# The first batch of an attention and mixture-of-experts kernel goes through the prologue in two halves

## The chip, the cores and the metric

The kernel runs on one core of one Trainium2 chip. The metric is the device time of one execution in microseconds (us), from the program's start to its end; the profile's span is the part of it from the first to the last instruction.

## The reference, cut to what matters

Four batches of 512 rows of 128 numbers go through a layernorm, an attention in segments, a projection and a layernorm with a residual, and then through a layer of eight experts (two per row) and a shared one.

```
B, M, D = (4, 512, 128)      H = 16, hd = 8, SEG = 128, DIL = 2, S = M // SEG = 4
qkv = layernorm(x) @ w_qkv.T
q, k, v = split by head, rows reordered by perm (a snake of width 23)
kd, vd = every second key and value of each segment of 128        # 64 keys a segment
scores = einsum('bhsqd,bhskd->bhsqk', q * hd**-0.5, kd)
attn   = softmax(scores);  o = einsum('bhsqk,bhskd->bhsqd', attn, vd)
x = x + layernorm(o @ w_out.T)
x = x + layernorm(moe(layernorm(x)))      # router, top 2 of 8 experts, shared gated expert
```

## The kernel before

Each engine has a program of its own, an order written out by hand, and semaphores tie them together. The work comes in three parts: a prologue that brings batch 0 (and the projections of batch 1) to the point where the attention can begin, a loop of three stages i = 0, 1, 2, in which the attention of batch i runs interleaved with the query scores of batch i + 1 and the projections of batch i + 2, and then the attention of batch 3 with the experts of all batches.

What a batch needs before its attention, in the names of the code:

- VectorE (DVE) takes the statistics of the four row tiles (`stats_x`: `bn_stats`, `bn_aggr`, one add), GpSimd (POOL) raises them to the power of -1/2 (`powers`), DVE makes the scaled negative mean (`neg_mean`), ScalarE (ACT) normalises the tiles (`normalise_x`, tile `XN`).
- TensorE (PE) transposes them (`x_T`). The products run in a number format that rounds its inputs, so each operand is split into a high part, copied by ACT (`x_high`, tile `xTh`), and a low part, the rest, subtracted by DVE (`x_low`, `xTl`); `split3` adds three products. `qkv` makes queries and keys, which are split again (`qk_high`, `qk_low`: `qch`, `qcl`, `kch`, `kcl`).
- `select_k` and `select_q` multiply by a 0/1 matrix `sel` and lay high and low parts of a group of four heads one under the other; ACT copies the results to `Ks` and `Qs` (`k_rows`, `q_rows`, one of the four query groups by DVE). DVE masks the keys by head into `Kb` (`k_blocks`, four instructions).
- `scores_q` gives scores whose row maxima DVE takes (`maxima`, tile `negm`); `max_split` splits them into `Mq`, PE transposes (`max_T`), ACT and DVE copy them into rows 96 to 127 of `Qs` (`max_rows`), where rows of `Kb` filled with ones (`kone`, made by ACT, spread by eight DMAs) meet them in `scores_k`. Its results are already less the maximum, and ACT takes the exponential (`exps`). `values` and `v_blocks` bring the values to `Vb`, `attend`, `attend_T` and `divide` end the attention.
- POOL copies every second column of `xTh` and `xTl` for the values (`key_columns`), and subtracts for the low parts of some weights (`w_low`: `rwl`, `gul`, `w1l`).

The order of DVE in the prologue is: statistics of batch 0, low part of the weights, `neg_mean(0, 0)`, the two copies to `sel`, statistics of batch 1, `x_low(0)`, `neg_mean(0, 1)`, `qk_low(0)`, two copies that put the ones into `Vb`, `k_blocks(0)`, statistics of batch 2, `q_rows(0)`, `maxima(0, 0)`, `neg_mean(0, 2)`, `x_low(1)`, `maxima(0, 1)`, `qk_low(1)`, `maxima(0, 2)`, statistics of batch 3, `maxima(0, 3)`, `max_split(0)`, `k_blocks(1)`, `neg_mean(0, 3)`; then the loop. PE's banks PA, PBk, PC, PD and the pairs S1, S2 are eight PSUM banks; in the prologue before, batch 0 uses PA, PBk and S1.

Of the kernel before, what the change touches and what calls it, by code (L numbers as in the profile page):

```python
# [26 lines left out]
HT = NT // 2  # L27
H, HD = 16, 8
G = 4
HG = H // G  # L30
KEYS = 64
KB = NT * KEYS
SNAKE = 23
# [56 lines left out]
def program(nc, x, w_qkvT, w_outT, router_w, w1, w2, gate_up, down, gate_w, xp, consts, out):  # L90
    with ExitStack() as ctx:
# [99 lines left out]
        ld_id, kdma = sem("ld_id"), sem("kdma")  # L191
# [33 lines left out]
        def _(sp):  # L225
            sp.dma_start(wqkv_n[:], w_qkvT.rearrange("d (c n) -> d c n", c=3)).then_inc(S["ld_wqkv"], 16)
            sp.dma_start(XP[:, 1], xp_v[1]).then_inc(ld_xp[1], 16)
            sp.dma_start(cst[:, P:C_END], consts[:, P:C_END]).then_inc(S["ld_cst"], 16)
# [12 lines left out]
            for u in range(2):  # L241
                for s in range(NT):
                    sp.dma_start(Kb[MROW:P, u, :, s].bitcast(F32), kone[MROW:P].bitcast(F32)).then_inc(kdma, 16)
# [12 lines left out]
        def _(pool):  # L256
# [11 lines left out]
            def key_columns(b):  # L268
# [3 lines left out]
                for to, src, done in ((xkh, xTh, "xh"), (xkl, xTl, "xl")):  # L272
                    pool.wait_ge(S[done], b + 1)
# [10 lines left out]

            def powers(k, b):

                pool.wait_ge(ve[k], b + 1)
                if k == 0 and b == 0:
                    pool.wait_ge(S["nhalf_set"], 1)
# [45 lines left out]
        def _(pe):  # L335
# [6 lines left out]

            def x_T(b):
                if b == 0:
                    pe.wait_ge(ld_id, 16)
                if b >= 1:
                    pe.wait_ge(S["qs_a"], 3 * b)
# [7 lines left out]
            def split3(out_, wh, wl, vh, vl):  # L355
                mm(out_, wh, vh, start=True, stop=False)  # L356
                mm(out_, wl, vh, start=False, stop=False)  # L357
                return mm(out_, wh, vl, start=False, stop=True)  # L358

            def qkv(b):  # L360
                pe.wait_ge(S["xh"], b + 1)
                pe.wait_ge(S["xl"], b + 1)
                if b == 0:
                    pe.wait_ge(S["wTh"], 1)
                    pe.wait_ge(S["wTl"], 1)
                else:
                    pe.wait_ge(S["vb"], 2 * b)
# [3 lines left out]
            def select_k(b):  # L371

                if b == 0:
                    pe.wait_ge(S["selr"], 2)
                pe.wait_ge(S["kh"], b + 1)
                pe.wait_ge(S["kl"], b + 1)
                for half in range(2):
                    if half == 1:
                        pe.wait_ge(S["qh"], b + 1)
                        pe.wait_ge(S["ql"], b + 1)  # L380
# [6 lines left out]
            def select_q(b, g):  # L387
# [3 lines left out]
                else:  # L391
                    pe.wait_ge(S["qs_a"], 3 * b + g - 1)
# [4 lines left out]
            def values(b):  # L397

                pe.wait_ge(S["qs_d"], b + 1)
# [8 lines left out]
            def scores_q(b, s, halves=(0, 1)):  # L408

                for half in halves:  # L410
                    n = (b * NT + s) * 2 + half
                    if half == 0:
                        pe.wait_ge(S["qs_a"], 3 * b + 2)
                        pe.wait_ge(S["kb_d"], HG * (b + 1))
                    else:
                        pe.wait_ge(S["qs_a"], 3 * b + 3)
                        pe.wait_ge(S["qs_d"], b + 1)
# [16 lines left out]
            def scores_k(b, s, halves=(0, 1)):  # L434

                for half in halves:
                    n = (b * NT + s) * 2 + half
                    pe.wait_ge(*((S["mev_d"], b + 1) if half else (S["mev_a"], 2 * b + 2)))
                    if b == 0 and s == 0 and half == 0:
                        pe.wait_ge(kdma, 16 * 2 * NT)  # L440
# [43 lines left out]
            def project(b):  # L484
# [3 lines left out]
                if b < B - 2:  # L488
                    pe.wait_ge(S["qs_a"], 3 * (b + 3))
# [921 lines left out]
```

## Time and profile before

| what | value |
|---|---|
| three runs | 181.8 us median (180.99 to 183.46) |
| the profiled execution, its time | 181.68 us |
| its span | 179.7 us |
| mean granted clock of PE | 0.943 |
| busy: PE, DVE, ACT, POOL | 153.4, 132.1, 112.8, 48.5 us |

The profiled execution lies within 0.1 us of the median of the runs; 2.0 us of it lie outside the span. An engine's busy time is a sum over parts with different limits, so a change to the prologue is read in the first 60 us alone.

### The profile page before, as it was taken

How to read it: one execution, taken by the hardware profiler on the slowest of the kernel's cores; microseconds unless marked ns; L12 is line 12 of the kernel's file. 1: busy time of each engine (PE TensorE's matmuls, PEld its weight loads, DVE VectorE, ACT ScalarE, POOL GpSimd, SP SyncE). 2: the span in 40 equal slices, each digit the busy share in tenths (PEclk: the TensorE clock that was granted, in tenths of full speed). 3: DMA queues.
4: the chain of work that ended last, by engine and by line, in shares of the span. 5: the costliest groups of instructions: out<-in, count | busy, mean ns of one | idle time of the engine just before them, and what ended most of it. 6: DMA issues, size and time to landing. Idle time of an engine off the chain costs nothing.

```text
span 179.7 us, 3601 instructions
## 1 busy us (share of the span) xinstructions
PE 153.4 (85%) x1176; PEld 127.3 (71%) x1176; DVE 132.1 (74%) x499; ACT 112.8 (63%) x264; POOL 48.5 (27%) x47
## 2 busy tenths in 40 slices
PE   6597788499868996699989999999999899999920
PEld 3144576298648975499758887889997899979920
DVE  1728758975496589747967896768999963996793
ACT  4354645977466656886378668953778377846803
POOL 4250220304300042002200220229843079402211
PEclk9967857999999999999789999999999999999996
DMA  5999400000000000000000000000000200010102
GB/s 168 284 290 229 87 2 0 4 0 2 4 0 0 4 0 0 0 4 0 5 2 0 4 0 0 4 0 2 0 4 0 60 0 5 0 58 0 44 18 58
DMA packets 10753, 6.03 MB, mean 34 GB/s; under 512 B 880, under 2 KB 10736, under 8 KB 10736
## 3 DMA queue, kind: packets, MB, share of 16 engines
q1 hardware_dynamic: 10064, 5.48, 13.0%
q10 hardware_dynamic: 672, 0.33, 0.6%
q8 instruction: 10, 0.16, 0.4%
q14 instruction: 7, 0.06, 0.1%
HBM read 3.71 MB, written 1.05 MB: 26 GB/s over the span
## 4 chain that ended last, share of the span: by engine, by line
PE 63%; DVE 22%; ACT 7%; issue 4%; DMA 2%; POOL 1%; POOLq 0%; ACTq 0%; DVEq 0%
PE bank L626 15%; PE bank L445 8%; PE bank L356 6%; PE bank L358 5%; PE bank L357 5%; DVE Kb L1064 5%; PE bank L422 4%; PE bank L462 4%; DVE negm L1087 3%; DVE ST L1014 2%; DMA XP<-in_x_snake 2%; PE bank L495 2%; DVE X L1235 2%; PE bank L475 2%; DVE qcl L1053 1%
## 5 line engine op out<-in xcount | busy, mean ns | idle before, releaser
L290 POOL TENSOR_TENSOR RS<-VE,nhalf 128x4 f32<-128x4 f32 x15 | 15.4, 1025 | 86.8 <-DVE VE L1019 86.8
L1235 DVE SCALAR_TENSOR_TENSOR X<-bank,CW,X 128x128 f32<-128x128 f32 x80 | 22.4, 342 | 7.8 <-PE bank L626 7.7
L1087 DVE TENSOR_REDUCE negm<-bank 128x8 f32<-128x512 f32 x32 | 20.6, 683 | 8.6 <-PE bank L422 8.6
L626 PEld LDWEIGHTS bank<-w2n,Pr 128*128 128x128 f32 x192 | 25.0, 191 | 2.0
L626 PE MATMUL bank<-w2n,Pr 128*128 128x128 f32 x192 | 25.2, 275 | 0.0
L810 ACT ACTIVATE Pr<-bank 128x512 f32<-128x512 f32 x32 | 17.9, 599 | 10.3 <-PE bank L445 10.3
L917 ACT ACTIVATE Pr<-bank 128x512 f32<-128x512 f32 x27 | 16.3, 604 | 11.9 <-PE bank L358 11.8
L445 PE MATMUL bank<-Qs,Kb 128*128 128x128 f32 x128 | 17.8, 276 | 0.3
L445 PEld LDWEIGHTS bank<-Qs,Kb 128*128 128x128 f32 x128 | 16.4, 192 | 1.6 <-issue 0.7
L356 PE MATMUL bank<-XH,w1h 128*128 128x512 f32 x32 | 15.1, 473 | 0.0
L306 POOL TENSOR_TENSOR Tm<-Tm 128x512 f32<-128x512 f32 x7 | 9.0, 1288 | 20.3 <-ACT Tm L932 20.3
L932 ACT ACTIVATE Tm<-bank,CW 128x128 f32<-128x128 f32 x44 | 12.5, 369 | 2.6 <-PE bank L626 2.6
L422 PE MATMUL bank<-Kb,Qs 96*128 96x256 f32 x64 | 13.0, 329 | 0.0
L358 PE MATMUL bank<-XL,w1h 128*128 128x512 f32 x32 | 12.6, 394 | 0.0
L357 PE MATMUL bank<-XH,w1l 128*128 128x512 f32 x32 | 12.6, 394 | 0.0
L283 POOL TENSOR_TENSOR EX<-base,DL 128x36 f32<-128x36 f32 x2 | 12.3, 6130 | 0.9 <-DVE DL L1136 0.9
L422 PEld LDWEIGHTS bank<-Kb,Qs 96*128 96x128 f32 x64 | 10.1, 214 | 2.2 <-issue 2.2
L1064 DVE TENSOR_SCALAR Kb<-Ks,cst 96x1024 fp32r<-96x1024 f32 x16 | 10.9, 744 | 0.8 <-ACT Ks L781 0.8
L462 PE MATMUL bank<-Pr,Vb 128*32 128x128 f32 x256 | 11.0, 293 | 0.0
L775 ACT ACTIVATE Qs<-bank 96x512 fp32r<-96x512 f32 x12 | 7.0, 591 | 4.5 <-PE bank L395 4.5
L394 PE MATMUL bank<-qch,sel 128*96 128x512 f32 x16 | 8.1, 508 | 1.1 <-ACT Qs L775 0.9
L626 PE MATMUL bank<-w2n,hs 128*128 128x128 f32 x64 | 8.7, 279 | 0.0
(142 smaller groups left out, 358.9 us busy)
## 6 DMA issues: line engine op xcount, KB each, us to landing
X<-in_L_attn_x SPq DMA_DIRECT2D x4, 256.0 KB, 5.1
Kb<-kone SPq DMA_DIRECT2D x8, 128.0 KB, 5.3
XP<-in_x_snake SPq DMA_DIRECT2D x3, 256.0 KB, 4.5
out<-XN SPq DMA_DIRECT2D x3, 256.0 KB, 2.3
w1n<-in_L_ffn_w SPq DMA_DIRECT2D x1, 512.0 KB, 5.2
w2n<-in_L_ffn_w SPq DMA_DIRECT2D x1, 512.0 KB, 6.5
XP<-in_x_snake ACTq DMA_DIRECT2D x1, 256.0 KB, 3.7
out<-XN SPq DMA_DIRECT2D x2, 128.0 KB, 1.8
```

What stands on the lines that cost most here:

```text
L356: mm(out_, wh, vh, start=True, stop=False)
L357: mm(out_, wl, vh, start=False, stop=False)
L358: return mm(out_, wh, vl, start=False, stop=True)
L422: i = mm(S1[n % 2][:, j * 256:(j + 1) * 256], Qs[0:MROW, b % 2, g, s * P:(s + 1) * P], Kb[0:MROW, b % 2, g, s], start=True, stop=True)
L445: i = mm(S2[s2_bank(n)][:, j * P:(j + 1) * P], Kb[:, b % 2, g, s, 2 * pr:2 * pr + 2], Qs[:, b % 2, g, s * P:(s + 1) * P], start=True, stop ...
L462: i = mm(PC[j * VW:(j + 1) * VW, (s % 2) * 2 * P + half * P:(s % 2) * 2 * P + (half + 1) * P], Vb[:, b % 2, s, half * 4 + j], Pr[:, n % 4, ...
L626: i = mm(ps[output_bank(n, s)][:, s * P:(s + 1) * P], lhs[:, s * P:(s + 1) * P], w, start=True, stop=True)
L810: A(Pr[:, n % 4], bank(S2[s2_bank(n)], 4), ACT.Exp).then_inc(S["ex"], 1)
L917: A((hs0 if b == 0 else hs)[:, k % 3 if k >= 0 else 3], ps[hidden_bank(n)][:], ACT.Silu).then_inc(S["sh"], 1)
L1064: V.tensor_scalar(Kb[0:MROW, b % 2, :, :, h].rearrange("p g s k -> p (g s) k"), Ks[0:MROW].bitcast(F32).rearrange("p g (s k) -> p (g s) k" ...
L1087: V.tensor_reduce(negm[:, b % 2, s, 8 * half:8 * half + 8], bank(S1[n % 2], 8, KEYS), AX.X, ALU.max, negate=True).then_inc(S["mx"], 1)
L1235: V.scalar_tensor_tensor(out=acc[:, b, t], in0=ps[output_bank(n)][:, t * P:(t + 1) * P], scalar=CW[:, b, t, k:k + 1], in1=acc[:, b, t], op ...
```

## The change

Batch 0 is cut into two halves of two segments each (256 rows, 128 keys). Its load comes in two DMAs, one on ACT's queue, one at the head of SP's; the constants come in one DMA on ACT's queue instead of two on two queues. Every step of batch 0 from the powers to the maxima has a form for one half (names with `_0`), and the halves have PSUM banks of their own: transposes in PA and PBk, keys in PD and S2[1], queries in PC and S2[0]. The counts of the later batches move by one or two. All four query groups of batch 0 are copied by ACT, in pairs.

Beside that the orders change. POOL makes the copies to `sel` (`select_rows`) and the ones in `Vb` (`value_ones`) instead of DVE. ACT makes `kone` before the high part of the weights, not after `x_high(0)`. DVE's statistics of batch 2 go behind `k_blocks(1)`, those of batch 3 into stage 0 of the loop ahead of `divide(0, 0)`, with `powers(0, 3)` on POOL now in the loop ahead of `w_low` for `w1l`; ACT's `normalise_x(2)` and `(3)` go into stage 0. The warm-ups of PE are 7 + 2 + 1 of 256 columns instead of 2 of 512, 1 of 256, 1 of 512. Each half of the key blocks' ones has its own semaphore (`kdma[u]`).

```diff
 sync
+            sp.dma_start(XP[:, 0, HT:NT], xp_v[0][:, HT:NT]).then_inc(ld_x0[1], 16)
             sp.dma_start(wqkv_n[:], ...)
             sp.dma_start(XP[:, 1], xp_v[1]).then_inc(ld_xp[1], 16)
-            sp.dma_start(cst[:, P:C_END], consts[:, P:C_END]).then_inc(S["ld_cst"], 16)
 gpsimd
-            powers(0, 0)
+            powers_0(0)
+            powers_0(1)
+            select_rows()
             powers(0, 1)
             key_columns(0)
+            value_ones()
+            key_columns(1)
             powers(0, 2)
-            key_columns(1)
-            powers(0, 3)
             w_low(rwl ...); w_low(gul ...)
             ...
                 if i + 2 < B:
                     key_columns(i + 2)
+                if i == 0:
+                    powers(0, 3)
                 ...
                 if i == 0:
                     w_low(w1l[:], w1n[:], w1h[:], S["w1hs"], 1, S["w1ls"])
 gpsimd, new functions
+            def powers_0(h):
+                t0, t1 = HT * h, HT * (h + 1)
+                pool.wait_ge(ve[0], h + 1)
+                nc.gpsimd.tensor_tensor(RS[:, 0, 0, t0:t1], VE[:, 0, 0, t0:t1], nhalf[:, t0:t1], ALU.pow)...
+            def select_rows():
+                pool.wait_ge(S["ld_cst"], 16)
+                nc.gpsimd.tensor_copy(sel[:, :, 0:2], eye).then_inc(S["selr"], 1)
+                nc.gpsimd.tensor_copy(sel[:, :, 4:8:2], eye).then_inc(S["selr"], 1)
+            def value_ones():
+                for u in range(2):
+                    nc.gpsimd.tensor_copy(Vb[:, u]..., cst[:, C_VB:C_VB + VW]...to_broadcast(...))
 tensor
-            warm_up(2)
-            warm_up(1, 256)
-            x_T(0)
-            warm_up(1)
-            qkv(0)
-            select_k(0)
-            for g in range(G):
-                select_q(0, g)
-            scores_q(0, 0, (0,))
+            warm_up(7, TH)
+            x_T_0(0)
+            warm_up(2, TH)
+            qkv_0(0)
+            x_T_0(1)
+            select_k_0(0)
+            qkv_0(1)
+            select_q_0(0, 0)
+            select_q_0(0, 1)
+            warm_up(1, TH)
+            scores_q(0, 0)
+            select_k_0(1)
+            select_q_0(1, 0)
+            select_q_0(1, 1)
+            scores_q(0, 1)
             values(0)
-            scores_q(0, 0, (1,))
             x_T(1)
-            scores_q(0, 1)
+            scores_q(0, 2)
             qkv(1)
-            scores_q(0, 2)
+            scores_q(0, 3)
             select_k(1)
-            scores_q(0, 3)
 scores_q
+                    if b == 0:
+                        pe.wait_ge(S["qs_a"], 2 * (s // HT) + half + 1)
+                        pe.wait_ge(S["kb_d"], HG * (s // HT + 1))
 scalar
-            act.dma_start(XP[:, 0], xp_v[0]).then_inc(ld_xp[0], 16)
-            act.dma_start(cst[:, 0:P], consts[:, 0:P]).then_inc(ld_id, 16)
+            act.dma_start(XP[:, 0, 0:HT], xp_v[0][:, 0:HT]).then_inc(ld_x0[0], 16)
+            act.dma_start(cst[:], consts).then_inc(S["ld_cst"], 16)
             A(warm[:], nhalf[:, 0:1], ACT.Exp)
+            act.wait_ge(S["ld_cst"], 16)
+            A(kone ...)
             act.wait_ge(S["ld_wqkv"], 16)
             A(wqkvh[:], wqkv_n[:], ACT.Copy).then_inc(S["wTh"], 1)
-            normalise_x(0); x_high(0); (kone); qk_high(0)
-            k_rows(0, 0); k_rows(0, 1); q_rows(0, 0 to 2)
+            normalise_x_0(0)
+            x_high_0(0)
+            normalise_x_0(1)
+            k_high_0(0)
+            q_high_0(0)
+            x_high_0(1)
+            k_rows_0(0)
+            k_high_0(1)
+            q_high_0(1)
+            q_rows_0(0, 0)
+            q_rows_0(0, 1)
+            k_rows_0(1)
+            q_rows_0(1, 0)
+            q_rows_0(1, 1)
             normalise_x(1)
             v_blocks(0)
             x_high(1)
             ...
-            normalise_x(2)
             for i in range(B - 1):
                 exps(i, 0)
+                if i == 0:
+                    normalise_x(2)
                 exps(i, 1)
                 attended(i, 0)
-                if i + 3 < B:
-                    normalise_x(i + 3)
                 ...
                 attended(i, 3)
+                if i == 0:
+                    normalise_x(3)
 vector
-            stats_x(0)
+            for h in range(2):
+                dve.wait_ge(ld_x0[h], 16)
+                stats(0, 0, ..., HT * h, HT * (h + 1))
             weights_low()
-            neg_mean(0, 0); select_rows(); stats_x(1); x_low(0); neg_mean(0, 1); qk_low(0); (ones of Vb)
-            k_blocks(0); stats_x(2); q_rows(0); maxima(0, 0); neg_mean(0, 2)
+            neg_mean_0(0)
+            spread(0, 1, ...)          # the bn_stats of batch 1
+            neg_mean_0(1)
+            gather(0, 1)               # its bn_aggr
+            x_low_0(0)
+            k_low_0(0)
+            q_low_0(0)
+            neg_mean(0, 1)
+            x_low_0(1)
+            k_blocks_0(0)
+            k_low_0(1)
+            q_low_0(1)
+            maxima(0, 0)
+            k_blocks_0(1)
+            maxima(0, 1)
             x_low(1)
-            maxima(0, 1)
+            maxima(0, 2)
             qk_low(1)
-            maxima(0, 2)
-            stats_x(3)
             maxima(0, 3)
             max_split(0)
             k_blocks(1)
-            neg_mean(0, 3)
+            stats_x(2)
             for i in range(B - 1):
                 max_rows(i)
                 q_rows(i + 1)
+                if i == 0:
+                    neg_mean(0, 2)
                 ...
                     qk_low(i + 2)
+                if i == 0:
+                    stats_x(3)
                 divide(i, 0)
+                if i == 0:
+                    neg_mean(0, 3)
                 maxima(i + 1, 3)
                 max_split(i + 1)
                 k_blocks(i + 2)
                 divide(i, 1)
```

## Rows read from the trace of the kernel before

**Rows 1.** The page, 40 equal slices: PE busy, granted clock, in tenths.

```profile
PE   6597788499868996699989999999999899999920
...
PEclk9967857999999999999789999999999999999996
```

**Rows 2.** The chain that ended last, first 60 us: start, us, what.

```profile
16.32 2.74 DVE Kb L1064 x4
...
29.68 0.78 DVE ST L1014 x4
...
30.86 1.29 DVE negm L1087 x2
...
54.42 0.66 PE bank L481 x4
```

**Rows 3.** The timeline, 0 to 22 us: start, us, instruction [idle before it].

```profile
3.61 0.52 ACT L832 ACTIVATE wqkvh<-wqkv_n 128x384 fp32r<-128x384 f32 x1 [0.34 <-DMA wqkv_n<-in_L_attn_w_qkv]
...
5.75 0.55 DVE L1030 TENSOR_TENSOR wqkvl<-wqkv_n,wqkvh 128x384 fp32r<-128x384 f32 x1
...
7.40 1.65 ACT L731 ACTIVATE XN<-XP,NM,RS 128x128 f32<-128x128 f32 x4 [3.27 <-DVE NM L1024]
...
9.61 0.60 ACT L739 ACTIVATE xTh<-bank 128x512 fp32r<-128x512 f32 x1 [0.56 <-PE bank L352]
10.23 1.05 ACT L836 ACTIVATE kone<-cst 32x1024 fp32r<-32x1024 f32 x1
...
10.27 0.65 POOL L274 CAST xkh<-xTh 128x512 fp32r<-128x512 f32 x1
...
13.32 0.38 ACT L757 ACTIVATE kch<-bank 128x256 fp32r<-128x256 f32 x1
13.93 0.41 DVE L1056 TENSOR_TENSOR kcl<-bank,kch 128x256 fp32r<-128x256 f32 x1
```

**Rows 4.** The timeline, 22 to 58 us.

```profile
22.56 0.84 ACT L794 ACTIVATE Vb<-bank,cst 128x256 f32<-128x256 f32 x2 [1.38 <-PE bank L405]
...
24.39 0.69 DVE L1049 TENSOR_TENSOR xTl<-bank,xTh 128x512 fp32r<-128x512 f32 x1 [0.72 <-ACT xTh L739]
...
26.84 0.60 ACT L753 ACTIVATE qch<-bank 128x512 fp32r<-128x512 f32 x1 [2.08 <-PE bank L358]
...
29.72 1.08 ACT L781 ACTIVATE Ks<-bank 96x512 fp32r<-96x512 f32 x2 [1.82 <-PE bank L384]
...
31.03 1.01 POOL L290 TENSOR_TENSOR RS<-VE,nhalf 128x4 f32<-128x4 f32 x1 [5.25 <-DVE VE L1019]
...
35.96 0.69 DVE L1073 CAST Qs<-Qs 32x1024 fp32r<-32x1024 f32 x1
...
44.09 2.38 POOL L266 TENSOR_TENSOR w1l<-w1n,w1h 128x1024 fp32r<-128x1024 f32 x1
...
50.54 0.19 DVE L1094 CAST Mq<-negm 128x64 fp32r<-128x64 f32 x1
```

**Rows 5.** The timeline where POOL and DVE overlap, at 32 us.

```profile
32.17 0.72 POOL L266 TENSOR_TENSOR gul<-gun,guh 128x256 fp32r<-128x256 f32 x1
32.17 0.77 DVE L1094 CAST Mq<-negm 128x64 fp32r<-128x64 f32 x1
```

**Rows 6.** DMA issues: KB each, us from issue to landing.

```profile
cst<-in_consts ACTq DMA_DIRECT2D x1, 64.0 KB, 4.2
```

**Rows 7.** Windows: us, busy PE PEld DVE ACT POOL, granted clock, DMA share, GB/s.

```profile
3.00:6.00 3.00, 2.88 (x5) 1.01 (x3) 1.48 (x10) 0.78 (x3) 0.08 (x1) 1.00 1.18 312
...
24.00:27.00 3.00, 2.40 (x8) 1.84 (x8) 1.89 (x3) 0.92 (x4) 1.28 (x2) 0.50 0.01 3
27.00:30.00 3.00, 2.70 (x16) 2.43 (x15) 2.53 (x7) 1.10 (x3) 0.00 (x0) 0.59 0.00 0
30.00:33.00 3.00, 1.09 (x8) 0.64 (x6) 2.90 (x12) 3.00 (x7) 1.86 (x3) 1.00 0.02 5
```

**Rows 8.** The chain further on: the same four matmuls at either clock.

```profile
80.12 0.67 PE bank L422 x4
...
88.17 1.15 PE bank L422 x4
```

More of the change, by code:

```diff
@@ L27 @@
 HT = NT // 2
+TH = T // 2
 H, HD = 16, 8
@@ L32 @@
 KB = NT * KEYS
+KH = KB // 2
 SNAKE = 23
@@ L190, in program @@
         stored = [sem(f"stored{b}") for b in range(B)]
-        ld_id, kdma = sem("ld_id"), sem("kdma")
+        ld_x0 = [sem(f"ld_x0_{h}") for h in range(2)]
+        kdma = [sem(f"kdma{u}") for u in range(2)]
         ident = cst[:, C_ID:C_ID + P]
@@ L272, in key_columns @@
                 for to, src, done in ((xkh, xTh, "xh"), (xkl, xTl, "xl")):
-                    pool.wait_ge(S[done], b + 1)
+                    pool.wait_ge(S[done], b + 2)
                     nc.gpsimd.tensor_copy(
@@ L341, in warm_up, with split3, x_T_0 @@
                     mm(S1[0][:, 0:width], Y[:, 0], Y[:].rearrange("p t d -> p (t d)")[:, 0:width], start=True, stop=True)
+            def split3(out_, wh, wl, vh, vl):
+                mm(out_, wh, vh, start=True, stop=False)
+                mm(out_, wl, vh, start=False, stop=False)
+                return mm(out_, wh, vl, start=False, stop=True)
+            def x_T_0(h):
+                if h == 0:
+                    pe.wait_ge(S["ld_cst"], 16)
+                for t in range(HT):
+                    pe.wait_ge(S["xn"], HT * h + t + 1)
+                    i = tp((PA, PBk)[h][:, t * P:(t + 1) * P], XN[:, 0, HT * h + t], ident)
+                i.then_inc(S["xT_ps"], 1)
@@ new lines, in qkv_0 @@
+            def qkv_0(h):
+                pe.wait_ge(S["xh"], h + 1)
+                pe.wait_ge(S["xl"], h + 1)
+                if h == 0:
+                    pe.wait_ge(S["wTh"], 1)
+                    pe.wait_ge(S["wTl"], 1)
+                t0, t1 = TH * h, TH * (h + 1)
+                split3((PD, S2[1])[h][:, 0:KH], wqkvh[:, 1], wqkvl[:, 1],
+                       xTh[:, t0:t1:2], xTl[:, t0:t1:2]).then_inc(S["kc"], 1)
+                split3((PC, S2[0])[h][:, 0:TH], wqkvh[:, 0], wqkvl[:, 0],
+                       xTh[:, t0:t1], xTl[:, t0:t1]).then_inc(S["qc"], 1)
@@ new lines, in select_k_0 @@
+            def select_k_0(h):
+                if h == 0:
+                    pe.wait_ge(S["selr"], 2)
+                pe.wait_ge(S["kh"], h + 1)
+                pe.wait_ge(S["kl"], h + 1)
+                for g in range(G):
+                    o = (PA, PBk)[h][0:MROW, g * KH:(g + 1) * KH]
+                    mm(o, sel[:, g, 4:7], kch[:, KH * h:KH * (h + 1)], start=True, stop=False)
+                    i = mm(o, sel[:, g, 5:8], kcl[:, KH * h:KH * (h + 1)], start=False, stop=True)
+                i.then_inc(S["ks_ps"], 1)
@@ new lines, in select_q_0 @@
+            def select_q_0(h, pair):
+                pe.wait_ge(S["qh"], h + 1)
+                pe.wait_ge(S["ql"], h + 1)
+                for j in range(2):
+                    o = ((PC, PD), S2)[h][pair][0:MROW, j * TH:(j + 1) * TH]
+                    mm(o, sel[:, 2 * pair + j, 0:3], qch[:, TH * h:TH * (h + 1)], start=True, stop=False)
+                    i = mm(o, sel[:, 2 * pair + j, 2:5], qcl[:, TH * h:TH * (h + 1)], start=False, stop=True)
+                i.then_inc(S["qs_ps"], 1)
@@ L353, in x_T @@
                 i.then_inc(S["xT_ps"], 1)
[L355 to L358, printed above, removed]
             def qkv(b):
[L361 to L367, printed above, removed]
+                pe.wait_ge(S["xh"], b + 2)
+                pe.wait_ge(S["xl"], b + 2)
+                pe.wait_ge(S["vb"], 2 * b)
                 split3(PBk[:], wqkvh[:, 0], wqkvl[:, 0], xTh[:], xTl[:]).then_inc(S["qc"], 1)
@@ L438, in scores_k @@
                     pe.wait_ge(*((S["mev_d"], b + 1) if half else (S["mev_a"], 2 * b + 2)))
-                    if b == 0 and s == 0 and half == 0:
-                        pe.wait_ge(kdma, 16 * 2 * NT)
+                    if b < 2 and s == 0 and half == 0:
+                        pe.wait_ge(kdma[b], 16 * NT)
                     if n >= 2:
@@ L830, in _ @@
             A(warm[:], nhalf[:, 0:1], ACT.Exp)
-            act.wait_ge(S["ld_wqkv"], 16)
-            A(wqkvh[:], wqkv_n[:], ACT.Copy).then_inc(S["wTh"], 1)
-            normalise_x(0)
-            x_high(0)
             act.wait_ge(S["ld_cst"], 16)
@@ L837, in _ @@
               .to_broadcast([P - MROW, G, HG, KEYS]), ACT.Copy).then_inc(S["kones"], 1)
-            qk_high(0)
-            k_rows(0, 0)
-            k_rows(0, 1)
-            for g in range(G - 1):
-                q_rows(0, g)
+            act.wait_ge(S["ld_wqkv"], 16)
+            A(wqkvh[:], wqkv_n[:], ACT.Copy).then_inc(S["wTh"], 1)
+            normalise_x_0(0)
[12 more added lines that the diff above has]
+            q_rows_0(1, 1)
             normalise_x(1)
```

164 lines of the change are left out of this document (101 added, 63 removed).

## The prediction

> **What bounds the kernel now.** I read the page's slices first: PE is busy nine tenths and more from about 36 us on, and poorly before that, with a granted clock that falls twice in the first 30 us [rows 1]. So the end is set by PE's queue once the loop is under way, and what the prologue gives is a shift of the point where that queue fills. Next the chain of waits up to 60 us, in order of time [rows 2]. It is not PE's: it goes from the landing of batch 0 through DVE, ACT and PE in turn, and DVE holds its longest pieces, the four key blocks of 2.74 us, the statistics of a later batch (1.18 us from 29.68 to 30.86) and the maxima behind them. Then the timelines of the same stretch [rows 3, 4], for what each hop costs. The reader should mark two points. One is 36.65 us, the end of DVE's copy of the maxima into `Qs` (35.96 + 0.69): with it the attention of batch 0 can run in full, and behind it PE is nearly always busy. The other is 54.42 us, where PE has waited for `divide(0, 1)` and the chain comes out of DVE's queue once more. What the change gains is counted at the first point, what it moves into the loop at the second.
>
> **The head.** Before, ACT splits the weights at 3.61 us and DVE their low part at 5.75 us, in cover of the landing and the power; ACT normalises at 7.40 [rows 3]. In the new order ACT waits for the constants, makes `kone` (1.05 us), and only then the high part (0.52), and DVE's `neg_mean_0(0)` is queued behind the low part (0.55) that waits for it. So the first normalisation hangs on the landing of the constants, and no longer on the load of x. They landed 4.2 us after their issue at 1.22, at 5.42, behind 256 KB of x in the same queue [rows 6]. Now 95 KB lie behind 128 KB: 223 KB instead of 320 KB; with two queues sharing the 312 GB/s seen from 3 to 6 us [rows 7] that is some 0.6 us sooner. I take 4.8 us; the ends are 4.1 and 5.4. Then 4.8 + 1.05 + 0.52 + 0.55 + 0.16 (the negative mean, about as long as before) + hops = 7.15 us for ACT's start, against 7.40. The half powers are done by then (statistics at about 4.4, one power up to 1.01 us for four columns [rows 4]). The seven warm-ups end before that and cost nothing; the two behind the first transposes may cost up to 0.8 us, which I hold for the range.
>
> **The halves.** From 7.15: two normalisations (half of 1.65) 7.98; transposes and hop 0.55, as from 9.05 to 9.61, 8.5; high part 0.38 and low part 0.41, at the durations of 256 columns [rows 3], 9.3; keys' product 10.0, their high and low parts (128 columns, between half of these and the whole; I take 0.3 and 0.3) 10.65; eight selections of about 0.11 and a hop 11.7; `Ks` for the first half (0.54, half of 1.08 for two of the same size [rows 4]) 12.25. Before, `Kb` began at 16.32 [rows 2], so at this point the halves are 4 us ahead. Beside that path ACT and DVE carry the second half: `xTl` of it ends at about 11.6. Key blocks of a half are four instructions of a size for which no row stands: 0.34 (half of the 0.68 that one costs within the 2.74) to 0.68; I take 0.37, 1.5 us for four, 13.75.
>
> Here POOL comes in. Released by `xTl` at 11.6 it copies `xkl` (about 0.65) and then runs `value_ones`, two copies of 1,024 columns, which at twice 0.65 for 512 columns [rows 3] are about 1.25 us each, from 12.3 to 14.8, right over the key blocks. What this does is seen at 32.17: DVE's copy to `Mq` took 0.77 us beside POOL's `gul`, which ran from 32.17 to 32.89; the same copy takes 0.19 alone [rows 4, 5]. DVE stood until POOL was done. But DVE's `xTl` out of PSUM at 10.24 was not slowed beside `xkh`, which ran from 10.27 [rows 3]. So the key blocks, SBUF to SBUF as the `Mq` copy is, lose none, one or both of the 1.25 us. I take one, since DVE may slip in between the two: end 15.0.
>
> The Trainium skill (SBUF — State Buffer, Who interferes with whom) says that GpSimd and a DVE copy or `tensor_scalar` in its two-port mode exclude each other for a whole instruction, and that whoever is first blocks the other. By that rule the trace agrees at 32.17, and the price here would be one or two `value_ones`, not a share of them.
>
> Onward, with the block: low parts of the second half 15.65; its key selection, 16.4; `Ks` 16.95; two pairs of `Qs` 18.05; `normalise_x(1)` (1.65) 19.8; `v_blocks` 0.84, 20.65; `xTh` 0.60, 21.25. ACT is the bound in this piece and DVE has 0.4 to 1.5 us of slack before `x_low(1)`, so one block costs 0.85 at this point, not 1.25, and two cost 2.05. `x_low(1)` begins at 21.25, where it was 24.39: 3.1 us gained. From there the order of before holds up to `Ks` of batch 1, with the low clock of before too: `qch` started at 26.84, `Ks` ended at 30.80 [rows 4], and 3.1 us sooner is 27.7. Beside it DVE takes only the last maxima and `max_split` (1.3 and 0.45, done at about 27.0). `k_blocks(1)` 27.7 to 30.4, statistics of batch 2 1.2, and the copy of the maxima 0.69: 32.3 us, against 36.65. Gain at the first point 4.4 us. Had PE its full clock here, some 1.1 us more would come: three products of 512 columns and eight selections go twice as fast. What it consists of: 3.1 up to `x_low(1)`; 0.6 of POOL's `gul` that no longer stands ahead of `Mq`; the rest maxima that now lie beside `Ks`. The statistics of batch 2 stand ahead of the copy where those of batch 3 stood ahead of the maxima: even. POOL's power for them might get ahead of that copy and hold it for 1.0 us; it came 0.17 us after DVE's next instruction at 30.86 and 31.03 [rows 2, 4], so I take nothing.
>
> **What is moved into stage 0.** ACT's `normalise_x(2)` between the exponentials takes the place that `normalise_x(3)` had, and `(3)` falls into ACT's idle time at 51 us: nothing, and 1.65 us if its cover is gone. DVE is another matter. The statistics of batch 3 (1.2 us) stand ahead of `divide(0, 0)` and lie on the chain that ends at 54.42. `neg_mean(0, 3)` waits for the power: 1.01 us less 0.7 of the division, 0.35 of a stall, and 0.15 itself, less the 0.15 that the old place gives back. Queued behind it are the maxima, `max_split`, the key blocks and `divide(0, 1)`, and PE waits for that. And `w_low` for `w1l`, 2.38 us on POOL, ran at 44.09 beside maxima out of PSUM [rows 4]; now it follows that power, in the old clock from 50.95 to 53.3. The copy to `Mq` would be due at 52.3 and stands until 53.3: 0.95 us, by the row at 32.17. Sum 1.2 + 0.35 + 0.15 + 0.95 = 2.7 us, roughly. PE had nothing but the end of `divide` to wait for there, so it passes in full.
>
> **The sum.** -4.4 + 2.7 = -1.7 us on the profiled execution's 181.68 us: 180.0. That run is the median of before but for 0.1 us, so the forecast stands for the median too.
>
> **The rivals.** First, POOL and DVE don't meet: `value_ones` comes later than I think, or the key blocks go first, and `w1l` starts after the `Mq` copy. Then 0.85 and 0.95 come off, 178.2; with the full clock up to 28 us besides, 177.1. For it speaks that my times are good to half a microsecond only; against it, that both overlaps are over 1 us wide.
>
> Second, the other side: the clock falls where PE is the bound. It is 0.50, which is 1.2 GHz of 2.4, from 24 to 27 us and for the most part of the next three [rows 7], after PE had worked in bursts with idle time between; such a spell costs little there, since DVE is the bound. In the new order PE waits from about 28.5 us to 32.3 for the copy of the maxima, with little but four selections. If the spell starts there, it holds for some 6 us the stretch in which PE is the bound: four matmuls take 1.15 against 0.67 us [rows 8], so 6.4 us at the low clock do the work of 3.7, and 2.6 us are lost: 182.6, just slower than before. It decides if the granted clock is 0.50 at 32 us. Before, PE was busy for 1.09 us of the three from 30 us and the clock stayed full [rows 7], which speaks against it.
>
> Third, the change doesn't bring the head forward: the constants land at 5.4 as before, or both copies block. That is +0.6 or +1.2: 180.6 to 181.8 with both. The first half would wait behind `kone`, and the halves would only pay in their overlap.
>
> **How the numbers follow.** My forecast, 180.0 with its own range 178.7 to 180.6: 0.42. No meeting of POOL and DVE, 176.8 to 178.7: 0.26. Late head or both blocks, 180.6 to 181.8: 0.14. The clock, 181.8 to 182.9: 0.08. Left, below 176.8 0.06 (the hops shorter than I count) and above 182.9 0.04. The range of 8 in 10 is 176.8 to 181.8. 2% is 3.6 us here, about what a measurement can tell from no change: below 178.1 is the larger part of the second case and the low rest, 0.25; above 185.4 hardly any, 0.03; between them 0.72.
>
> **What would show it.** Right: ACT's first `XN` near 7.2 us, after `kone` and `wqkvh`; the first `Kb` instruction near 12.3 and one of the first half's four drawn out to over 1 us beside POOL's `Vb`; `x_low(1)` near 21; the copy of the maxima ending near 32; `Mq` of batch 1 taking about 1 us beside `w1l`; the output transposes (54.42 before) near 52.7. Wrong: `Kb` at 0.37 throughout, a granted clock of 0.50 behind 32 us, or a gain at the copy of the maxima that is not given back by stage 0.

## The result, and the profile after

The changed kernel took 188.5 us in the median of four runs (187.61 to 190.27), the kernel before 181.54 (180.99 to 183.46): a ratio of 1.042, 95% interval 1.035 to 1.049. It is slower by 4%, where I had forecast 180.0 us and a range up to 181.8. Six more runs of the same kernel, taken later, must be told with it, since the number can't be understood without them: two of the ten lie at 181.84 and 182.98 us with a mean granted clock of 0.972 and 0.952, the other eight at 187.61 to 191.39 with 0.908 to 0.927. The profiled execution (190.27 us, span 188.5) is one of the eight.

The slices of the page after, PE's busy share and its granted clock (before: [rows 1]):

```profile
PE   6986886899864899759998999999999899999930
```

```profile
PEclk9998769655896599999969999999999999999995
```

A slice is 4.7 us (4.5 before). Before, the clock was back at full speed by slice 8 and stayed there up to slice 19; after, it is low in slices 8 to 11, where PE is busy eight tenths and more, and again in slices 13 and 14. The dip near 90 us (slices 20 and 21 before, 21 after) is in both. The windows around the first of these (us, busy time of PE PEld DVE ACT POOL, clock, DMA share, GB/s):

```profile
34.00:51.00 17.00, 16.98 (x117) 14.99 (x118) 5.40 (x10) 8.29 (x19) 2.97 (x5) 0.60 0.01 1
51.00:62.00 11.00, 5.45 (x40) 3.40 (x39) 10.39 (x25) 5.78 (x13) 3.35 (x2) 0.83 0.00 0
```

And the chain of waits after, in order of time (start, us, what), to be laid beside [rows 2]:

```profile
1.25 3.50 DMA cst<-in_consts
...
12.46 3.53 DVE Kb L1173 x4
...
29.24 2.74 DVE Kb L1212 x4
31.97 0.78 DVE ST L1125 x4
...
33.27 0.70 DVE Qs L1221
...
51.00 0.69 DVE qcl L1201
...
54.41 2.32 DVE NM L1181
...
61.85 1.11 PE bank L548 x4
```

The reader can cut the run in four with this. The copy of the maxima ends at 33.97 us, against 36.65 before: 2.7 us won. `qcl` of batch 2 begins at 51.00. Before it was at 47.56, as this row of its timeline shows:

```profile
47.56 0.69 DVE L1053 SCALAR_TENSOR_TENSOR qcl<-bank,qch 128x512 fp32r<-128x512 f32 x1 [2.35 <-ACT qch L753]
```

So the stretch between took 17.0 us instead of 10.9: 6.1 lost, with PE busy for 16.98 of 17.00 us and its clock at 0.60 in the mean. From `qcl` to the output transposes it is 10.85 us instead of 6.86 (54.42 before [rows 2]): 4.0 lost, with DVE busy. From there to the end 126.65 instead of 125.28: 1.4 lost. -2.7 + 6.1 + 4.0 + 1.4 = 8.8 us, which is the difference of the spans, 188.5 less 179.7.

The timeline of the prologue and of stage 0 shows the two places where DVE stood (start, us, instruction [idle before it]):

```profile
7.27 0.88 ACT L801 ACTIVATE XN<-XP,NM,RS 128x128 f32<-128x128 f32 x2 [0.90 <-DVE NM L1144]
...
12.46 3.52 DVE L1173 TENSOR_SCALAR Kb<-Ks,cst 96x512 fp32r<-96x512 f32 x4 [0.28 <-ACT Ks L822]
...
12.85 2.46 POOL L308 COPY Vb<-cst 128x1024 f32<-128x1024 f32 x2
...
18.17 1.67 DVE L1173 TENSOR_SCALAR Kb<-Ks,cst 96x512 fp32r<-96x512 f32 x4 [0.23 <-ACT Ks L822]
...
54.35 2.36 POOL L269 TENSOR_TENSOR w1l<-w1n,w1h 128x1024 fp32r<-128x1024 f32 x1
54.41 2.32 DVE L1181 SCALAR_TENSOR_TENSOR NM<-MV,RS 128x4 f32<-128x4 f32 x1 [0.41 <-POOL RS L315]
```

The first half's key blocks took 3.52 us beside POOL's two copies, the second half's 1.67 with POOL idle. One by one, the four of the first half and POOL's two copies:

```profile
12.46 0.72 DVE L1173 TENSOR_SCALAR Kb<-Ks,cst 96x512 fp32r<-96x512 f32 x1 [0.28 <-ACT Ks L822]
13.11 1.29 DVE L1173 TENSOR_SCALAR Kb<-Ks,cst 96x512 fp32r<-96x512 f32 x1
14.32 1.27 DVE L1173 TENSOR_SCALAR Kb<-Ks,cst 96x512 fp32r<-96x512 f32 x1
15.52 0.47 DVE L1173 TENSOR_SCALAR Kb<-Ks,cst 96x512 fp32r<-96x512 f32 x1
12.85 1.26 POOL L308 COPY Vb<-cst 128x1024 f32<-128x1024 f32 x1
14.06 1.25 POOL L308 COPY Vb<-cst 128x1024 f32<-128x1024 f32 x1
```

The second block ends 0.29 us behind the first copy (14.40 and 14.11), the third 0.28 us behind the second copy (15.59 and 15.31). So one block did pass between the copies, and the next one stood for the second copy. And `neg_mean(0, 3)`, an instruction of 0.16 us, took 2.32 beside `w1l` and ended with it (56.73 and 56.71).

### The profile page after: what moved, and what is told of

Read it like the earlier page. It is cut to its first block, busy times and chain, and to the rows that moved or that the text cites. A ratio compares the mean times of both kernels' runs of the same rounds, so it can differ in the third digit from the quotient of the medians.

```text
span 188.5 us, 3688 instructions
## 1 busy us (share of the span) xinstructions
PE 161.9 (86%) x1210; PEld 138.3 (73%) x1210; DVE 135.7 (72%) x503; ACT 114.1 (61%) x268; POOL 52.6 (28%) x52
## 3 DMA queue, kind: packets, MB, share of 16 engines
q1 hardware_dynamic: 10192, 5.58, 12.3%
## 4 chain that ended last, share of the span: by engine, by line
PE 63%; DVE 21%; ACT 5%; issue 4%; DMA 2%; POOL 1%; ACTq 0%; POOLq 0%; DVEq 0%
PE bank L697 14%; PE bank L512 8%; PE bank L373 5%; PE bank L489 5%; PE bank L375 5%; PE bank L374 5%; DVE Kb L1212 4%; PE bank L529 4%; DVE negm L1235 2%; PE bank L562 2%; DVE Kb L1173 2%; DMA cst<-in_consts 2%; DVE X L1391 2%; PE bank L542 2%; DVE ST L1125 2%
## 5 line engine op out<-in xcount | busy, mean ns | idle before, releaser
L315 POOL TENSOR_TENSOR RS<-VE,nhalf 128x4 f32<-128x4 f32 x14 | 14.6, 1045 | 84.9 <-DVE VE L1133 84.9
L913 ACT ACTIVATE Pr<-bank 128x512 f32<-128x512 f32 x32 | 18.1, 597 | 12.5 <-PE bank L512 12.3
L512 PE MATMUL bank<-Qs,Kb 128*128 128x128 f32 x128 | 20.0, 298 | 0.8 <-DVE Qs L1221 0.5
L512 PEld LDWEIGHTS bank<-Qs,Kb 128*128 128x128 f32 x128 | 18.6, 214 | 2.3 <-issue 0.9
L489 PE MATMUL bank<-Kb,Qs 96*128 96x256 f32 x64 | 14.2, 354 | 1.5 <-DVE Kb L1173 1.5
L489 PEld LDWEIGHTS bank<-Kb,Qs 96*128 96x128 f32 x64 | 11.1, 239 | 4.2 <-issue 4.2
L286 POOL TENSOR_TENSOR EX<-base,DL 128x36 f32<-128x36 f32 x2 | 12.3, 6128 | 0.9 <-DVE DL L1284 0.9
L529 PE MATMUL bank<-Pr,Vb 128*32 128x128 f32 x256 | 11.7, 307 | 0.0
L905 ACT ACTIVATE AVs<-bank 128x256 f32<-128x256 f32 x16 | 6.3, 395 | 5.8 <-PE bank L529 5.8
L542 PE MATMUL bank<-cst,AVs 128*128 128x128 f32 x32 | 7.2, 312 | 2.5 <-ACT AVs L905 1.5
L529 PEld LDWEIGHTS bank<-Pr,Vb 128*32 128x32 f32 x256 | 6.7, 119 | 3.2 <-issue 2.9
L370 PE MATMUL bank<-Y 128*128 128x256 f32 x20 | 7.7, 551 | 1.4 <-DVE Y L1315 1.4
```

Source lines behind the costliest of these rows:

```text
L489: i = mm(S1[n % 2][:, j * 256:(j + 1) * 256], Qs[0:MROW, b % 2, g, s * P:(s + 1) * P], Kb[0:MROW, b % 2, g, s], start=True, stop=True)
L512: i = mm(S2[s2_bank(n)][:, j * P:(j + 1) * P], Kb[:, b % 2, g, s, 2 * pr:2 * pr + 2], Qs[:, b % 2, g, s * P:(s + 1) * P], start=True, stop ...
L529: i = mm(PC[j * VW:(j + 1) * VW, (s % 2) * 2 * P + half * P:(s % 2) * 2 * P + (half + 1) * P], Vb[:, b % 2, s, half * 4 + j], Pr[:, n % 4, ...
L913: A(Pr[:, n % 4], bank(S2[s2_bank(n)], 4), ACT.Exp).then_inc(S["ex"], 1)
```

## The experiments

Times are medians with the lowest and highest run, ratios are to the kernel before, run again beside each (medians of 181.57 to 182.77 us). "The spell" is a granted clock of 0.50 that begins right behind the copy of the maxima and lasts near 14 us. Where the clock was low is known of the profiled run of each kernel alone; the other runs are counted by their time and mean clock.

**The kernel once more.** No edit, six runs.

> The changed kernel itself once more, unaltered. Its four runs so far (187.6 to 190.3 us) all had a mean granted clock of 0.908 to 0.927. Another kernel that differs from it in one step of POOL (w1l) had two runs at 179.4 and 179.9 us with a clock of 0.97 to 0.98, and two at 186.6 and 186.9 with 0.927. Theory clock: whether the low spell falls on the loop differs from run to run, so this kernel has fast runs too, near 182 us at a clock of 0.97, beside those near 188 us. Rival: its order brings the spell in every run; then all runs lie above 187 us.

181.84, 182.98, 187.62, 187.74, 190.14 and 191.39 us, with clocks of 0.972, 0.952, 0.926, 0.926, 0.908 and 0.917. There are two kinds of runs, and the profiled one is without the spell at 0.50 (182.98 us, span 181.2). Its windows, and behind them those of the first profile, PE alone (us, busy time and matmuls, clock, DMA share, GB/s):

```profile
36.00:42.00 6.00, 6.00 (x59) 1.00 0.01 3
42.00:49.00 7.00, 4.79 (x56) 1.00 0.00 0
49.00:61.00 12.00, 8.65 (x55) 0.72 0.00 0
```

```profile
36.00:42.00 6.00, 6.00 (x41) 0.50 0.01 1
42.00:49.00 7.00, 7.00 (x43) 0.56 0.01 2
49.00:61.00 12.00, 7.29 (x66) 0.89 0.00 0
```

Same kernel, same order: 59 matmuls in six microseconds, or 41. In the second profile the copy of the maxima ends at 32.70 us and `qcl` begins at 43.60, 10.90 us later, as before the change to a hundredth. So the 6.1 us are the clock's, and not one of them is the order's; `normalise_x(2)` between the exponentials, the rival in the expectation below, costs nothing here. The 10.85 us behind `qcl` are there in the second profile too, so those 4.0 us belong to the order. This run won 3.95 us up to the copy of the maxima, gave 4.0 back by the output transposes, and lost 1.5 more behind them, where its clock is 0.72.

**Warm-ups, all five and in parts.** Three kernels add matmuls of 256 columns into the idle bank PD:

```diff
             scores_q(0, 2)
 ...
+            warm_pd(2)                        # "early"
             qkv(1)
 ...
                 select_q(i + 1, 1)
+                if i == 0: warm_pd(1)         # "late"
 ...
-                scores_k(i, 0)
+                scores_k(i, 0, (0,)); warm_pd(2); scores_k(i, 0, (1,))    # "late", i == 0
```

> Edit: the changed kernel with five warm-up matmuls of 256 columns more, into PD, which is free there: two ahead of qkv(1), one behind select_q(1, 1), two between the halves of scores_k(0, 0). Theory clock: the stretch from the copy of the maxima to qch of batch 2 (33.96 to 51.00 us, 17.0 us, where the kernel before took 10.9) is long because PE's granted clock is 0.50 from 34 to 48 us; if PE does more in the gaps ahead of it the clock stays up, the stretch falls to 11 to 13 us and the time by 4 to 6 us, to 183 to 185 us. Theory order: the stretch is long because ACT's normalise_x(2) stands between the exponentials; then the time stays at 188 to 190 us, with the stretch above 15 us even at full clock.

> Edit: the changed kernel with three of the five added warm-ups: one behind select_q(1, 1), two between the halves of scores_k(0, 0); not the two ahead of qkv(1). If the spell in the loop hangs on what PE does right ahead of it (28 to 34 us), most runs lie near 182 us. If the earlier gap counts as well, most runs stay at 187 us and above.

> Edit: the changed kernel with two of the five added warm-ups, those ahead of qkv(1), not the three later ones. If the spell in the loop hangs on what PE does from 28 to 34 us, most runs stay at 187 us and above; if the gap at 22 to 24 us counts, most lie near 182 us.

All five: 182.05 us (181.45 to 190.53, ten runs), ratio 1.005 (1.000 to 1.011); seven of the ten at 182.3 or less, one (190.53, clock 0.928) with the spell. The late three: 184.4 (183.06 to 193.7, four runs), one with the spell; the profiled run (184.29) is without it, but has a clock of 0.63 from 49 to 61 us. The early two: 188.3 (181.89 to 189.86), three of four with it, the profiled one among them. What PE did ahead of the point, in the windows of the kernel with all five and then with the early two:

```profile
28.00:30.00 2.00, 1.24 (x5) 1.00 0.00 0
30.00:32.00 2.00, 1.75 (x11) 1.00 0.00 0
32.00:34.00 2.00, 2.00 (x18) 1.00 0.01 4
34.00:38.00 4.00, 4.00 (x47) 1.00 0.02 4
```

```profile
28.00:30.00 2.00, 1.12 (x4) 1.00 0.00 0
30.00:32.00 2.00, 1.09 (x6) 1.00 0.00 0
32.00:34.00 2.00, 1.96 (x12) 0.73 0.00 0
34.00:38.00 4.00, 4.00 (x31) 0.50 0.01 2
```

What PE does right around the copy of the maxima makes the spell more or less likely: two runs of 14 have it with the late warm-ups, 11 of 14 without. It doesn't fix it: a run of any of these kernels can fall either way.

**Who holds DVE.** One kernel gives the ones of `Vb` back to DVE, in two of its gaps, one restores the order of `w1l` on POOL.

```diff
 gpsimd
-            value_ones()                      # e2: on DVE, ahead of weights_low() and behind gather(0, 1)
 ...
                 if i == 0:
+                    w_low(w1l[:], w1n[:], w1h[:], S["w1hs"], 1, S["w1ls"])    # e3
                     powers(0, 3)
 ...
-                    w_low(w1l[:], w1n[:], w1h[:], S["w1hs"], 1, S["w1ls"])    # e3
```

> Edit: the ones of Vb are made by DVE in two gaps of its prologue (ahead of the low part of the weights, and behind the statistics of batch 1) instead of by POOL. Theory port: DVE's first key blocks take 3.5 us instead of 1.7 because POOL's two copies hold them up; they fall to 1.7 and x_low(1) begins 1 to 1.9 us sooner than at 23.18. The time falls by 1 to 2 us if the clock falls in the same places, else by whatever the clock makes of it. Rival: half-size key blocks cost 0.9 us each by themselves (strided halves); then they stay at 3.5 us.

> Edit: on POOL the low part of w1 goes ahead of powers(0, 3), as it did before the change, not behind. Theory port: DVE's neg_mean(0, 3) took 2.32 us instead of 0.15 because POOL's 2.36 us subtraction ran at the same time; it falls to 0.15 and the time by about 2.2 us, to some 186.3. Rival: the wait only moves to another instruction of DVE (the maxima wait for PE at its low clock), and the time falls by less than 0.5 us.

The first: 185.2 us, from 180.66 to 190.11, two of four runs with a clock near 0.915. The second: 183.3, from 179.44 to 186.87, two of four at 0.927. The medians only count the spells; the traces decide. This is the first kernel's DVE:

```profile
12.19 1.90 DVE L1172 TENSOR_SCALAR Kb<-Ks,cst 96x512 fp32r<-96x512 f32 x4 [0.28 <-ACT Ks L821]
...
20.15 0.69 DVE L1196 TENSOR_TENSOR xTl<-bank,xTh 128x512 fp32r<-128x512 f32 x1 [0.84 <-ACT xTh L844]
```

and this the second's:

```profile
47.58 0.16 DVE L1180 SCALAR_TENSOR_TENSOR NM<-MV,RS 128x4 f32<-128x4 f32 x1 [0.41 <-POOL RS L315]
```

The key blocks fell from 3.52 to 1.90 us, not to the 1.67 of the second half, since POOL still copies `xkl` beside the first of them, and `x_low(1)` came at 20.15, 1.6 us sooner than the 21.76 of the second profile above. `neg_mean` fell from 2.32 to 0.16 us, and the output transposes came 8.7 us behind `qcl` instead of 10.85. Before the change it was 6.86; the 1.8 us that are left are the statistics of batch 3 and the wait for their power.

**All three, and the two of POOL alone.**

> Edit: all three at once. If the clock's 4 to 6 us, the 1 to 2 of the first key blocks and the 2.2 of w1l add up, the time is 178.5 to 181.5 us, at or below the kernel before. If only the clock stays down, 184 to 186.

> Edit: the changed kernel with the two mends of POOL and DVE (ones of Vb, w1l) but without the added warm-ups. Theory clock: it has two kinds of runs, near 178 us at a clock of 0.97 and near 185 us at 0.92, where the kernel with the warm-ups had 176.9 to 178.5 in four runs. Rival: the warm-ups did nothing, and all runs lie at 177 to 179 us.

With the warm-ups 177.7 us (176.92 to 178.53), without them 184.4 (183.89 to 186.64, clocks 0.914 to 0.933). All four runs without them have a low clock, and the profiled one has the spell (0.50 from 31.0 to 44.7 us): what DVE gains is lost to the clock. The rival of the second expectation, that the warm-ups did nothing, fell.

**The statistics.** The next kernels move what the change had put on DVE's chain into waits that DVE has anyway in stage 0:

```diff
             k_blocks(1)
-            stats_x(2)                                # e15, e13
             ...
                 q_rows(i + 1)
+                if i == 0: stats_x(2)                 # e15, e13
                 maxima(i + 1, 0)
                 maxima(i + 1, 1)
+                if i == 0: stats_x(3)                 # e16, e13
                 ...
-                if i == 0: stats_x(3)                 # e16, e13
                 divide(i, 0)
```

with `neg_mean(0, 2)` behind `maxima(1, 0)` and `normalise_x(2)` behind `attended(0, 0)` where batch 2 is moved.

> Edit: the kernel with all three mends (warm-ups, ones of Vb, w1l), and the statistics moved: those of batch 2 behind q_rows(1), those of batch 3 behind maxima(1, 1), where DVE waits for PE; normalise_x(2) behind attended(0, 0). They stood on the chain for 1.2 us ahead of the copy of the maxima and for 1.5 us ahead of divide(0, 0). Theory: both come off, 177.7 less 2.0 to 2.7 gives 175.0 to 175.7 us. Rival: ACT's Ks and PE set these points as well, and under 1 us comes off.

> Edit: the changed kernel, without added warm-ups and with POOL as it is, but the statistics of batch 2 behind q_rows(1), those of batch 3 behind maxima(1, 1), and normalise_x(2) behind attended(0, 0). Theory: the gap ahead of the copy of the maxima is 1.2 us shorter, so the spell falls on the loop in fewer runs: most lie at 180 to 182 us. Rival: the halves themselves, which bring the loop forward and leave PE idle in the prologue, make the spell; then most runs stay above 186 us.

> Edit: the same with the ones of Vb on DVE and w1l ahead of powers(0, 3): the 176.8 us kernel less its five warm-ups. Theory: with the gap shorter the warm-ups are hardly needed: 176 to 178 us at 0.97 and more. Rival: it needs them, and runs near 184 us at 0.93 are seen.

> Edit: the changed kernel with the statistics of batch 2 alone behind q_rows(1), and normalise_x(2) behind attended(0, 0). Theory: this is the gap that makes the spell; without it most runs lie at 179.5 to 181 us with a clock of 0.96 and more, as neg_mean(0, 3) still waits 2.3 us for w1l. Rival: the gap is no cause, runs near 187 us stay.

> Edit: the changed kernel with the statistics of batch 3 alone behind maxima(1, 1). It lies behind the point where the spell starts, so it can't prevent it: two kinds of runs stay, each about 4 us below those of the changed kernel (1.2 of the statistics, 0.4 of the wait and 2.3 of the collision with w1l): near 178 and near 184 us. Rival: the spell goes with this step; then all runs lie at 177 to 179 us.

On the kernel with all mends: 176.8 us (176.08 to 176.97), only 0.9 won where 2.0 to 2.7 were expected; in its profiled run the constants landed late, and `kone` began at 5.51 us instead of 4.66. The traces also say why the move gives less than both statistics together. Counted from the first key blocks, the copy of the maxima ends 1.26 us sooner than without the move (16.82 us behind them instead of 18.08), but `qcl` of batch 2 comes at the same distance (29.11 and 29.10): the stretch between the two grew from 11.0 to 12.3 us. What is won, 1.75 us, lies behind `qcl` (6.94 us to the output transposes instead of 8.69) and is batch 3's. The rival, that other things set the first point as well, holds for batch 2. On the changed kernel with no other mend: 176.9 us (176.14 to 178.00), ratio to before 0.970 (0.961 to 0.980). That is 11 us less than the changed kernel's median, and 5 to 6 less than its two runs without the spell, by a move of eighteen short instructions of DVE (nine a batch) and what follows them, where 180 to 182 us were expected; I had not seen that `w1l` finds its place with it: it runs at 40.12 us there, beside maxima. With the ones and `w1l` mended: 176.6 (174.79 to 180.68), one run of four at a clock of 0.948.

Batch 3 alone: 176.2 us (176.09 to 184.64), three runs of four at a clock of 0.988 and one with the spell, 8.4 us above. Batch 2 alone: 183.5 (181.72 to 186.88, eleven runs), where 179.5 to 181 were expected; two of them near 186.8. The profiled run of batch 2 alone is one of these two (186.88 us, clock 0.917), and it is without the spell: its low stretch begins at 48.5 us, behind `qcl`, and lasts 17 us. Its windows, and the last of them for batch 3 alone:

```profile
34.00:48.00 14.00, 12.50 (x128) 1.00 0.01 2
49.00:61.00 12.00, 9.38 (x46) 0.50 0.00 0
```

```profile
49.00:61.00 12.00, 11.27 (x109) 1.00 0.00 1
```

So there is a second gap: PE waits for DVE behind `qcl`, and the clock falls after that wait too. Moving batch 3 closes it: the output transposes of that kernel start at 49.73 us, 6.9 behind its `qcl` at 42.80, as before the change. It takes 3.9 us off the chain and the loss behind it as well, 5.6 us in all (176.2 against 181.84 in runs without the first spell). Moving batch 2 gives nothing by itself in such runs. It seems to make the first spell rare, at most 1 of 11 runs instead of 8 of 10, but a time near 187 us can also come from the second gap, as that of the profiled one does. And the kernel with batch 3 alone differs from the changed one only behind the point where the spell starts, so I had expected the spell in most of its runs; it had it in one of four by the times. Four runs say little of how often a spell comes.

**The halves by themselves, and the kernel before with warm-ups.** The kernel before got the warm-ups in its own gaps, and in a second version the moved statistics too.

> Edit: the kernel before with seven warm-ups of 256 columns more in PE's gaps of the prologue: one ahead of select_k(0), two ahead of qkv(1), one ahead of select_k(1), three ahead of max_T(0). Theory clock: the spells at 0.50 up to 29 us go, at a price of about 1.1 us in the products of qkv(1) and select_k(1); the time is 179.5 to 181 us, the clock 0.97 or more, and the runs lie close together. Rival: the extra work stands in the way and nothing is won: 181 to 183 us.

> Edit: the kernel before, without halves, with the added warm-ups and with the statistics of batches 2 and 3 and their normalisations moved into DVE's waits of stage 0, as in the fastest kernel so far (176.8 us). It says what the halves are worth by themselves. Theory: the halves bring x_low(1) about 3 us forward and it passes to the end, so this kernel needs 178.5 to 180 us. Rival: the statistics were all of it, and this one reaches 177 us.

Warm-ups alone: 182.05 us (179.84 to 184.34), ratio 1.000 (0.994 to 1.005). The profiled run (179.89) kept its full clock from 14 to 173 us and had the output transposes at 53.25, 1.2 us sooner than before, but the median doesn't move; what the clock gives and what the warm-ups take can't be told apart in it. With the statistics moved: 178.7 (177.4 to 179.33), ratio 0.986 (0.978 to 0.994). Against 176.8 of the same with halves (the e7 kernel), the halves and what came with them (the loads, the place of `kone`, POOL's copies to `sel`) are worth 1.9 us, and the output transposes start at 50.81 against 49.15, 1.7 us apart.

**The head, and the best.** `kone` on ACT behind the query rows of the first half:

```diff
-            act.wait_ge(S["ld_cst"], 16); A(kone ...)     # ahead of wqkvh
 ...
             q_rows_0(0, 1)
+            act.wait_ge(S["ld_cst"], 16); A(kone ...)
             k_rows_0(1)
```

> Edit: the fastest kernel so far, with kone behind the query rows of the first half on ACT instead of ahead of the high part of the weights. The first normalisation then no longer hangs on the landing of the constants: it should start near 5.9 us instead of 7.2, and 1.0 to 1.3 us come off, to 175.5 us, if ACT has room for kone at 15 us. Rival: PE's seven warm-ups, which end at 7.5 us, stand in the way of the transposes, and only 0.3 us come off.

> Edit: the changed kernel with the statistics moved, the ones of Vb on DVE, w1l ahead of powers(0, 3), and kone behind the query rows of the first half; no added warm-ups. If the 1.3 us of the head add to the others: 173.5 to 175 us in most runs, with one in some at a lower clock 2 to 5 us above.

On the 176.8 us kernel: 175.5 (174.8 to 176.37), 1.3 us off. The first normalisation, in the last kernel:

```profile
4.17 0.52 ACT L933 ACTIVATE wqkvh<-wqkv_n 128x384 fp32r<-128x384 f32 x1 [0.91 <-DMA wqkv_n<-in_L_attn_w_qkv]
6.45 0.88 ACT L799 ACTIVATE XN<-XP,NM,RS 128x128 f32<-128x128 f32 x2 [1.76 <-DVE NM L1142]
```

6.45 us, and not 5.9: DVE's `neg_mean_0(0)` stands behind its copy of ones and POOL's power. The last, with halves, moved statistics, both mends of POOL, this head and no warm-up: 175.6 us (174.95 to 175.89), ratio 0.969 (0.962 to 0.976). It beats the kernel before by 3% and the changed one by 7%.

## Why the prediction was wrong

**The head** was right. 7.15 us was worked out, 7.27 measured; the constants landed at 4.75 (4.8 was taken) and ACT did wait for them. `neg_mean_0(0)` took 0.35 us, beside POOL's copies to `sel`, where 0.16 was taken; the sum held all the same.

**The halves** were right in kind. `Kb` began at 12.46 (12.25). I had charged one of POOL's two copies and kept both for the range. DVE did slip in between, as I had reckoned, but with one block, and the next stood for the second copy: both blocked. `x_low(1)` came at 21.76 us in the second profile and 23.18 in the first, where 21.25 was said; the second number has PE at 0.50 in the prologue. The gain at the copy of the maxima was 3.95 us in the second profile, for 4.4 forecast. Half-size key blocks cost 0.42 each, within the bounds of 0.34 and 0.68.

**What is moved into stage 0** is the first step that failed, in its size. I added 1.2 + 0.35 + 0.15 + 0.95 = 2.7; 4.0 was measured. The term mis-sized is the last: I let `neg_mean(0, 3)` pass in 0.15 us and put the collision with `w1l` at the copy to `Mq`, 0.95 us. But `neg_mean` starts in the very moment in which POOL ends the power and goes on to `w1l`, and it stood for 2.32 us. The copy to `Mq` took 0.20 us, as it does alone. Restoring POOL's order brought 2.15 us back, and the 1.8 that stay are the other three terms, which add up to 1.7. I had taken from the trace that a copy of DVE collides, and that DVE reading PSUM doesn't; that `neg_mean` reads two operands in SBUF I did not weigh. The Trainium skill (SBUF — State Buffer, Who interferes with whom) names that case: an instruction of DVE with two inputs in SBUF contends with one of GpSimd that reads SBUF, and the ports they share are an exclusive lock. The trace agrees, at 2.32 us beside 2.36.

So the sum without the clock was -3.95 + 4.0, no gain, where I had -1.7. That alone would have given 181.7 us, within the range. The two runs without the spell lie at 181.84 and 182.98.

**The clock** is the step that made the range fail. The sum has no term for it. The mechanism was the second rival, at the place that I gave: PE waits for the copy of the maxima with little to do, and behind it the clock is at 0.50. I gave it 0.08 and it came in eight runs of ten; and I priced it at 2.6 us, from a spell of 6.4, where it lasts 14 us and costs 6.1. The reason against it, that PE had idled in a like way before and kept its clock, was weak: one profiled run says nothing on how often a thing goes the other way.

What the change did to PE's waiting ahead of that point shows in these rows, the first of the kernel before, the second of the changed one:

```profile
33.26 0.66 PE L431 MATMUL bank<-cst,Mq 128*128 128x128 f32 x4 [2.17 <-DVE Mq L1096]
34.02 0.74 PE L512 MATMUL bank<-Qs,Kb 128*128 128x128 f32 x4 [0.51 <-DVE Qs L1221]
```

In all, PE waits less there than before: of the six us up to the end of the copy it was busy for 4.01 in the first profile and for 2.97 before, where one wait alone was 2.17 us and the clock stayed full. What is new is the wait of 0.51 us for the copy itself, inside `scores_k(0, 0)`. It comes from a step that I had booked as even, the statistics of batch 2 in the place of those of batch 3. For DVE's queue it was even; but those of batch 3 had stood ahead of the last maxima, and those of batch 2 stand right ahead of the copy. By times and clocks, 20 of 30 runs of the kernels whose profile has that wait have the spell, and at most 3 of 38 of the others made from the changed kernel (batch 2 alone left out, since of its two runs near 187 us one has none and the other wasn't profiled). That ties the spell to the wait; it doesn't say by what. And stage 0's added 4.0 us of DVE made a second gap with a low stretch of its own, which costs 1.4 to 1.5 us behind the output transposes in the two profiles of the changed kernel and which no step of mine had.

**Still open.** What decides in one run whether the spell comes isn't shown. Of the six us up to the end of the copy, PE was busy for 4.01 in the first profile and the spell came; in the second for 3.89, and it didn't. The kernel before isn't free of such times either: of its 60 runs three lie at 187.2, 187.97 and 188.69 us, with clocks of 0.928 to 0.932; no profile of them is kept.

## What to carry to other kernels

When a step is moved on one engine, count what it does to the idle time of PE right ahead of a stretch that PE bounds, and not only to the queue it is moved in: a new wait of 0.5 us there went with a low clock that cost 6.1 us here in most runs, three times what the halves are worth (1.9 us). Ask of every instruction of DVE with one or two operands in SBUF what POOL starts in that moment; a 0.16 us instruction behind a wait on POOL meets POOL's next one by construction. And where the clock can go either way, take several runs with their clocks before a median is read: the order of `w1l` alone moved the median from 188.5 to 183.3 us, where its trace shows 2.15 us.

## What the runs showed of the hardware that was not expected

The low clock outlasts the idle time ahead of it by far, and it stays low while PE is busy without a pause: from 36 to 42 us of the first profile PE was busy for 6.00 us of 6.00 at 0.50, from 42 to 49 for 7.00 of 7.00 at 0.56. The same kernel on the same inputs had it in eight runs of ten.

DVE and POOL took turns, one instruction at a time: with POOL's two copies in a row (1.26 and 1.25 us), one of DVE's waiting key blocks ended 0.28 to 0.29 us behind each copy, and the four took 3.52 us instead of 1.67.

A short instruction of DVE with two operands in SBUF stood in three places of the first profile for the instruction that POOL was running: `neg_mean`, 0.14 to 0.16 us by itself, took 0.35 beside the copies to `sel` (it ended at 7.23 us, as they did), 0.62 beside `xkh` and 2.32 beside `w1l`.
